# A quarter of the column terms by products over runs instead of gathers, and one comparison for a group's one-hot

## What is computed

```python
for l in range(3):
    f1 = relu(x[row] @ nb_W[l] + nb_b[l])
    f2 = relu(x[col] @ self_W[l] + self_b[l])
    h = relu(concatenate([f1, f2], axis=1) @ att1_W[l] + att1_b[l])
    log_alpha = (h @ att2_W[l] + att2_b[l])[:, 0]
    mask = clip(sigmoid(log_alpha) * (ZETA - GAMMA) + GAMMA, 0.0, 1.0)
    rowsum = segment_sum(mask, row) + 1e-06
    d_inv_sqrt = clip(rowsum ** (-0.5), 0.0, 10.0)
    vals = mask * d_inv_sqrt[row] * d_inv_sqrt[col]
    x = segment_sum(vals[:, None] * x[col], row)
    out = out + x
x = layernorm(x_in + out)
```

## Time and profile before

| | |
|---|---|
| median of 3 runs | 12707.59 us (12700.92 to 12740.07) |
| span of the profiled execution | 9111.0 us; no other time of that execution is given |
| median less span | 3596.6 us |
| PE, PEld busy | 5650.8 us, 5151.5 us |
| DVE, ACT, POOL busy | 6736.5 us, 3666.1 us, 5960.7 us |
| three layers' phase A | 6274.8 us of the span |
| three layers' phase B | 1907.1 us of the span |
| granted clock, mean | 0.623 |

### The profile page before, as it was taken

The page is one execution under the profiler, slowest core; times in us unless marked ns, Lnnn a source line. Parts: engine busy times, 40 slices in busy tenths (PEclk is TensorE's granted clock), DMA queues, the critical chain, the costliest instruction groups (busy, mean ns, idle before and its releaser), DMA issues.

```text
span 9111.0 us, 203370 instructions
## 1 busy us (share of the span) xinstructions
PE 5650.8 (62%) x43467; PEld 5151.5 (57%) x43630; DVE 6736.5 (74%) x29039; ACT 3666.1 (40%) x8663; POOL 5960.7 (65%) x6294
## 2 busy tenths in 40 slices
PE   3135555555558996555555557998555555555996
PEld 1135555545548885555555556887555555555886
DVE  8877777777777877777777777877777777776788
ACT  0013322322227883322322325885322322323886
POOL 0017777777775656777777776665777777776664
PEclk7565555555558996555555557998555555555998
DMA  1014444444456664444444446665444444445665
GB/s 24 0 48 135 132 130 131 132 130 130 133 128 206 213 206 130 132 131 130 132 130 131 132 130 176 210 212 156 132 130 130 133 130 131 132 130 146 213 211 161
DMA packets 1122388, 1272.27 MB, mean 140 GB/s; under 512 B 648596, under 2 KB 652724, under 8 KB 1122356
## 3 DMA queue, kind: packets, MB, share of 16 engines
q1 hardware_dynamic: 922676, 903.51, 32.1%
q0 software_dynamic: 199680, 368.45, 16.7%
HBM read 868.11 MB, written 403.23 MB: 140 GB/s over the span
## 4 chain that ended last, share of the span: by engine, by line
POOL 44%; issue 23%; PE 22%; DVE 8%; DMA 1%; ACT 1%; POOLq 0%; DVEq 0%; ACTq 0%; SPq 0%
POOL got L526 22%; PE bank L552 12%; POOL k_hot L526 11%; POOL g_hot L526 10%; PE bank L685 6%; DVE acc L946 2%; DVE acc L947 2%; PE bank L653 1%; PE bank L690 1%; PE bank L610 1%; PE bank L601 1%; PE bank L576 1%; DMA k_x<-kept_x 1%; DMA k_hot<-qx_table,index 0%; DVE acc L909 0%
## 5 line engine op out<-in xcount | busy, mean ns | idle before, releaser
L653 PE MATMUL bank<-p_all,onehot_t 128*128 x10032 | 2301.5, 424 | 1752.4 <-issue 1731.8
L653 PEld LDWEIGHTS bank<-p_all,onehot_t 128*128 128x128 f32 x10032 | 2186.8, 330 | 1803.4 <-issue 1803.4
L526 POOL DMA_INDIRECT got<-qx_table,index x2496 | 2376.4, 952 | 784.9 <-issue 780.3
L539 POOL DMA_INDIRECT got<-y_table,index x1248 | 1187.3, 951 | 798.8 <-issue 431.5
L798 ACT ACTIVATE small<-small 128x8 f32<-128x8 f32 x624 | 130.2, 209 | 3813.9 <-DVE small L1080 3813.9
L526 POOL DMA_INDIRECT k_hot<-qx_table,index x1248 | 1181.3, 947 | 393.7 <-issue 377.5
L526 POOL DMA_INDIRECT g_hot<-qx_table,index x1248 | 1185.6, 950 | 380.6 <-issue 380.6
L552 PE MATMUL bank<-mask,onehots 128*128 128x3 bf16 x4992 | 669.8, 184 | 986.1 <-DVE mask L1091 986.1
L552 PEld LDWEIGHTS bank<-mask,onehots 128*128 128x128 bf16 x4992 | 516.0, 104 | 1250.7 <-issue 1145.5
L1118 DVE SCALAR_TENSOR_TENSOR p_all<-iota_b,col_hi,bank 128x104 f32<-128x104 bf16 x3768 | 953.9, 317 | 341.5 <-PE bank L685 335.4
L1056 DVE TENSOR_SCALAR onehots<-iota_b,rows_b 128x128 bf16<-128x128 bf16 x5016 | 888.7, 280 | 48.0
(11 more groups left out here) (167 smaller groups left out, 8859.7 us busy)
## 6 DMA issues: line engine op xcount, KB each, us to landing
onehot_t<-look_hot SPq DMA_DIRECT2D x474, 256.0 KB
row_hot<-onehots SPq DMA_DIRECT2D x468, 256.0 KB, 3.6
k_x<-col_rows SPq DMA_DIRECT2D x318, 256.0 KB, 3.6
kept_x<-got SPq DMA_DIRECT2D x312, 256.0 KB
look_hot<-k_x SPq DMA_DIRECT2D x312, 256.0 KB, 2.1
hot_in<-row_hot SPq DMA_DIRECT2D x312, 256.0 KB
k_x<-kept_x SPq DMA_DIRECT2D x312, 256.0 KB
look_new<-row_hot SPq DMA_DIRECT2D x159, 256.0 KB
```

The costliest lines, as they stand in the source:

```text
L526: pool.indirect_dma_start(got[j][:, k, :], None, qx_table, bass.IndirectOffsetOnAxis(ap=index[j][:, k:k + 1], axis=0)).then_inc(a_got[j], 16)
L539: pool.indirect_dma_start(got[j][:, k, 0:HID], None, y_table, bass.IndirectOffsetOnAxis(ap=index[j][:, k:k + 1], axis=0)).then_inc(g_got[j ...
L653: last = mm(bank_p[h][:, k, :], onehot_t[h][:, k, :], p_all[:, ds(ids[k], 1), :].rearrange("p o d -> p (o d)"), start=True, stop=True)
```

## The change

**Fewer gathers.** The fourth group of each quad (j = 3) no longer gathers its Q. Its 1024 edges are cut into runs, stretches of one tile whose columns lie in one block of nodes. After the sort by row and column, the groups are ranked by their number of runs, and the 52 with the fewest are moved to the fourth place of the quads; at most 72 runs, here slots, stand for each. A slot's product multiplies a one-hot of the lanes of its edges (`slot_hot`, zero for edges of other runs) by the block of Q that the slot names, kept in SBUF as `q_res`, and adds to `bank[7]` at its tile. Block and tile of three slots are packed in one int32 word, which PE reads into a register and takes apart (`column_terms`). SP broadcasts the slots' lanes to all partitions (`load_slots`), DVE compares them with the partition number (`build_slots`). Nine rounds of eight slots make a quad's 72: rounds 0 to 2 in the group j = 0, 3 to 5 in j = 1, 6 to 8 in j = 2.

**One comparison.** A group has one one-hot, `hot[j]`, from `build_onehot`, for both of its uses.

**Besides.** The sort key also holds the column's block; finding the runs (nine times MAX and MATCH_REPLACE), ranking, and 36 gathers of column rows run once ahead of the layers. `block_of` and `spot_of` become rows of one int32 tile, `tile_at`. acc holds `q_res` in phase A, and POOL clears it by one memset ahead of phase B, in place of ACT step by step.

```diff
+    ROUNDS = 9
+    SLOTS = ROUNDS * U
+    SLOT_BITS, PER_WORD = 10, 3
+    WORDS = SLOTS // PER_WORD
+    RUNS = TILES + BLOCKS * (BLOCKS - 1)
+    ALL_GROUPS = 2 * PARTS
+    GROUP_EDGES = U * PARTS
+    PICKS = SLOTS // 2
+    CHUNK = PICKS // 3
...
-        block_of = sb("block_of", [1, TILES + AHEAD], mybir.dt.int16)
-        spot_of = sb("spot_of", [1, TILES + U], I32)
+        tile_at = sb("tile_at", [64, TILES + AHEAD], I32)
+        block_of, spot_of = tile_at[0:1, :], tile_at[32:33, :]
...
-        hot_a, hot_b = ([onehots[:, h * U:(h + 1) * U, :] for h in (first, first + 1)] for first in (0, 2))
+        hot = [onehots[:, j * U:(j + 1) * U, :] for j in range(4)]
...
+                def load_slots(b, r, made):
+                    if made is not None:
+                        sp.wait_ge(x_made, l * (ROUNDS * QUADS) + (b * ROUNDS + made))
+                        sp.sem_inc(sp_go, 1)
+                    sp.dma_start(slot_in[r % 3], slot_lanes[ds(b * SLOTS + r * U, U), :].rearrange("k e -> (k e)")
+                                 .partition_broadcast(PARTS)).then_inc(x_in[r % 3], 16)
...
+                        if j == 0:
+                            sp.wait_ge(x_used[0], l * (slots_used(0) * QUADS) + b * slots_used(0))
+                            sp.sem_inc(sp_go, 1)
+                            sp.dma_start(slot_word[0:1, :], slot_words[ds(b, 1), 1, :]).then_inc(w_in, 16)
+                            for r in range(3):
+                                load_slots(b, r, 0 if r == 0 else None)
                         load_columns(b, j + 2)
-                        sp.wait_ge(a_hotb, l * (GROUPS + 1) + (b * 4 + (j + 1)))
+                        sp.wait_ge(a_hot, l * (GROUPS + 2) + (b * 4 + (j + 1)))
                         sp.sem_inc(sp_go, 1)
                         sp.dma_start(row_hot[ds((b * 3 + j) * PARTS, PARTS), :],
-                                     hot_b[j % 2].rearrange("p k m -> p (k m)")).then_inc(a_hotst[j % 2], 16)
+                                     hot[j].rearrange("p k m -> p (k m)")).then_inc(a_hotst[j], 16)
+                        if j < 2:
+                            for r in (3 * j + 3, 3 * j + 4):
+                                load_slots(b, r, r - 2)
                         sp.wait_ge(a_got[j], (l * QUADS + b + 1) * GOT)
                         sp.sem_inc(sp_go, 1)
                         sp.dma_start(kept_x[ds((b * 3 + j) * PARTS, PARTS), :].rearrange("p (k d) -> p k d", k=U),
...
+            pool.wait_ge(s_place, 1)
+            for h in range(2):
+                pool.indirect_dma_start(
+                    sorted_keys, bass.IndirectOffsetOnAxis(ap=ranks_i[:, 2, h:h + 1], axis=0),
+                    sorted_of[:, h * GROUP_EDGES:(h + 1) * GROUP_EDGES], None
+                ).then_inc(s_scat, 16)
+            pool.wait_ge(s_nodest, 16)
+            pool.wait_ge(s_unpacked, 1)
+            for i in range(PICKS):
+                pool.indirect_dma_start(
+                    picked_rows[i // CHUNK][:, i % CHUNK * PARTS:(i % CHUNK + 1) * PARTS], None, node_rows,
+                    bass.IndirectOffsetOnAxis(ap=pick_row[:, i:i + 1], axis=0)
+                ).then_inc(s_picked[i // CHUNK], 16)
             pool.wait_ge(s_edges, 1)
...
-                    for j in range(4):
-                        pool.wait_ge(a_idx[j], l * (QUADS + (j < 3)) + (b + 1))
+                    for j in range(3):
...
+                pool.wait_ge(m_rows, l + 1)
+                pool.sem_inc(pool_go, 1)
+                pool.memset(acc[:, :, :], 0.0).then_inc(k_zero, 1)
...
+                        p_block = p_all[:, ds(ids[k], 1), :].rearrange("p o d -> p (o d)")
+                        if read:
+                            last = mm(bank_p[h][:, k, :], onehot_t[h][:, k, :], p_block, start=True, stop=True)
+                        else:
+                            last = plus(bank[7][:, k * HID:(k + 1) * HID], onehot_t[h][:, k, :], p_block)
...
+                def column_terms(b, j):
+                    n = l * QUADS + b
+                    if j == 0:
+                        pe.wait_ge(n_q, node_done(l, 0, NODE_STEPS - 1))
+                        pe.wait_ge(w_in, (n + 1) * 16)
+                        pe.sem_inc(pe_go, 1)
+                    pe.load(word, slot_word[0:1, j * U:(j + 1) * U])
+                    for r in range(3 * j, 3 * j + 3):
+                        pe.wait_ge(x_made, n * ROUNDS + (r + 1))
+                        for i in range(U):
+                            at, part = divmod((r - 3 * j) * U + i, PER_WORD)
+                            bits = pe.snap(word[at], min_val=0, max_val=BASE - 1) >> SLOT_BITS * part
+                            k = bits & U - 1
+                            s = nc.s_assert_within((bits >> 3) & PARTS - 1, 0, NB - 1,
+                                                   skip_runtime_bounds_check_because="a column's block is below BLOCKS")
+                            last = plus(bank[7][:, ds(k * HID, HID)], slot_hot[r % 2][:, i, :],
+                                        q_res[:, ds(s, 1), :].rearrange("p o d -> p (o d)"))
+                        last.then_inc(x_used[r % 2], 1)
...
-                with pe.Fori(0, GROUPS // 2) as b:
-                    for j in range(2):
-                        g = b * 2 + j
-                        row_terms(1 - j, g + 1, a_sum, l * GROUPS + g)
-                        turn_hot(j, g + 2)
-                        at = [pe.snap(r, min_val=0, max_val=BLOCKS - 1) for r in blk[j]]
-                        pe.wait_ge(a_hotb, l * (GROUPS + 1) + (g + 1))
+                with pe.Fori(0, QUADS) as b:
+                    for j in range(4):
+                        g = b * 4 + j
+                        if j == 2:
+                            column_terms(b, j)
+                            row_terms(1, g + 1)
+                        else:
+                            row_terms(1 - j % 2, g + 1, a_sum, l * GROUPS + g)
+                        turn_hot((j + 2) % 4, g + 2)
+                        if j == 0:
+                            pe.wait_ge(a_sum, l * GROUPS + g)
+                            clear(bank[7])
+                        if j < 2:
+                            column_terms(b, j)
+                        at = [pe.snap(r, min_val=0, max_val=BLOCKS - 1) for r in blk[j % 2]]
                         pe.wait_ge(a_m3, l * GROUPS + (g + 1))
                         for k in range(U):
-                            last = plus(bank_r[:, ds(at[k] * 4, 3)], hot_b[j][:, k, :], mask3[j][:, k, :])
...
-                        to = (j + 3) % 4
-                        act.wait_ge(a_add[to], l * QUADS + (b + (j > 0)))
-                        if to < 3:
-                            act.wait_ge(a_kept[to], (l * QUADS + (b + (j > 0))) * 16)
-                        a.copy(index[to][:, :], col_id[:, ds((g + 3) * U, U)]).then_inc(a_idx[to], 1)
+                        if j > 0:
+                            to = j - 1
+                            act.wait_ge(a_add[to], l * QUADS + (b + 1))
+                            act.wait_ge(a_kept[to], (l * QUADS + (b + 1)) * 16)
...
+            for r in range(ROUNDS):
+                eight = picks[:, 0, r * U:(r + 1) * U]
+                link(v.max(eight, pair[r % 2]))
+                link(v.match_replace(pair[(r + 1) % 2], eight, pair[r % 2], 0.0))
...
+                    v.tensor_copy(q_res[:, of_step(s), :], bank[4 + j % 2][:, :].rearrange("p (b d) -> p b d", d=HID))
...
-                def build_hot(to, rows, g, n, free, signal, stored=None):
-                    v.tensor_copy(rows[:, :], row_lo[:, ds(g * U, U)]).then_inc(a_rows, 1)
-                    dve.wait_ge(*free)
-                    if stored is not None:
-                        dve.wait_ge(stored[0], stored[1] * 16)
-                    dve.wait_ge(a_rows, l * (2 * GROUPS + 3) + (n + 1))
-                    for k in range(U):
-                        last = v.tensor_scalar(to[:, k, :], iota_b[:, :], rows[:, k:k + 1], None, ALU.is_equal)
-                    last.then_inc(signal, 1)
+                def build_hot(j, g, summed_up, stored):
+                    dve.wait_ge(a_row, l * (GROUPS + 1) + summed_up)
+                    if j < 3:
+                        dve.wait_ge(a_hotst[j], (l * QUADS + stored) * 16)
+                    build_onehot(hot[j], row_lo[:, ds(g * U, U)]).then_inc(a_hot, 1)
+                def build_slots(b, r):
+                    h = r % 2
+                    dve.wait_ge(x_in[r % 3], (l * (3 * QUADS) + (b * 3 + (r // 3 + 1))) * 16)
+                    dve.wait_ge(x_used[h], l * (slots_used(h) * QUADS) + (b * slots_used(h) + r // 2))
+                    v.tensor_scalar(slot_hot[h].rearrange("p k m -> p (k m)") if h == 0 else
+                                    slot_hot[h][:, :, :].rearrange("p k m -> p (k m)"),
+                                    slot_in[r % 3], part_f[:, :], None, ALU.is_equal).then_inc(x_made, 1)
+                dve.wait_ge(s_lanest, 96)
```

(24 more changed lines are left out.)

253 lines of the change are left out of this document (199 added, 54 removed).

## The result

The changed kernel takes 16,987.65 us (median of 4 runs, 16,966.37 to 17,021.72), the kernel before, beside it, 12,709.72 us (4 runs, 12,700.92 to 12,740.07): a ratio of 1.3366, 95% interval 1.3344 to 1.3388. I had forecast slower, 15,990 us, in a range that ended at 16,900. The side was right, the size 998 us short, and the time lies 88 us outside the range.

What follows compares the result with a forecast made beforehand. Phase A was taken as bound by POOL's gathers before and PE's sequencer after: (60.5 - 40.2) us x 156 quads + 115 = +3280 us on the 12,707.6 us median, 15,990 us; range 12,700 to 16,900.

Steps and rivals of the forecast that it cites:

- What bounds now: Phase A of the kernel before: bound by POOL's 32 gathers a quad, 40.2 us a quad.
- Register instructions, 94 to 106 ns each: PE's sequencer: five ahead of each slot product make a slot 0.525 us, 72 slots 37.8 us a quad.
- The array is not the limit: PE's array in the slots: 0.46 us a product at the lower clock, 0.24 at the upper, below 0.525 a slot.
- POOL and DMA are hidden: Phase A after: POOL's 24 gathers take 30.2 us a quad, DMA gains about 1.8 MB in 60 us; neither bounds.
- The int32 load: PE's load of eight block numbers: 591 ns instead of 2222 ns as int16, a gain of 1.6 us a group.
- The quad of 60.5 us: Phase A after: sequencer 57.9 us plus 2.6 of array time a quad, range 59.4 to 62.6, against 40.2 before.
- the array's own time: Last two groups of a quad, where no slots follow: adds 1.5 us at the upper clock, 4.7 at the lower; 2.6 taken.
- The single comparison is worth nothing: DVE in phase A: one comparison saves 8 us a quad, but PE's sequencer hides it, so no gain in time.
- The prologue, +105: Work ahead of the layers, with 36 gathers on POOL: 70 to 140 us more, 105 taken.
- The 3597 us: Timed median minus profiled span of the kernel before: assumed around the span or in unchanged parts, so the change adds 3280 us.
- Rival 1: The missing 3597 us are POOL's gathers, each slower in timed runs: centre 12,750 us, chance 0.22.
- Rival 3: The missing time is spread evenly, all engines slower by 1.395 in timed runs: 17,280 us, chance 0.1.

Runs made afterwards that it cites:

- e4: Changed kernel with one slot product a round (nine a quad) in place of eight, everything else kept: 12,771.17 us, ratio 1.003.
- e18: Changed kernel with 36 semaphore increments more a quad on TensorE's own queue: 17,525.36 us, ratio 1.3776.
- e3: Changed kernel with the 72 slot products at fixed addresses, without word loads or register instructions ahead of them: 14,128.37 us, ratio 1.1092.
- e2: Kernel before with only the single comparison in place of eight for each group's one-hots: 12,237.36 us, ratio 0.9611.
- e14: Changed kernel with the single comparison undone (a cast and eight comparisons a group again): 17,364.96 us, ratio 1.3644.
- e11: Changed kernel with 128 semaphore increments a queue ahead of the layers, moving all later code: 17,270.1 us, ratio 1.3506.
- the second profile: Kernel before, unchanged, timed and profiled again: 12,739.34 us, ratio 1.0006, span 12,718.5 us.
- e5: Kernel before with TensorE's phase A loop written over a quad (four groups) instead of two groups: 12,700.15 us, ratio 0.9992.
- e15: Kernel before with VectorE's phase A loop written over two quads: 12,719.94 us, ratio 0.9995.
- e9: Kernel before with 64 semaphore increments ahead of the layers on each of five queues, moving later code: 12,793.07 us, ratio 1.0003.
- e10: Kernel before with 128 semaphore increments ahead of the layers on each of five queues, moving later code: 12,810.31 us, ratio 1.0018.
- e12: Changed kernel with TensorE's phase A loop written over two quads: 17,025.14 us, ratio 1.3388.
- e6: Kernel before with 32 semaphore increments more a quad on ScalarE: 12,707.92 us, ratio 0.9995.
- e7: Kernel before with 24 semaphore increments more a quad on SyncE: 12,717.9 us, ratio 1.0.
- e16: Changed kernel with 36 semaphore increments more a quad on ScalarE: 17,050.13 us, ratio 1.341.
- e17: Changed kernel with 36 semaphore increments more a quad on VectorE: 17,062.28 us, ratio 1.3411.

## Why the prediction was right in direction and short in size

*What bounds now* failed for the timed runs. "Phase A is bound by POOL's 32 gathers" holds in the execution of the earlier trace rows, and there alone. In an execution like the timed ones a quad takes 54.3 us, not 40.2, POOL waits, VectorE is first in the chain, and in e4 a quarter fewer gathers won nothing.

*Register instructions, 94 to 106 ns each.* About right: 93 ns net in e18, and in the undisturbed slots of the packed trace (from 2063.4 us) the plain and fused ones of L676 mostly start 92 to 104 ns before the next instruction. A slot came to 0.576 us against 0.525, mostly since the first fused operation of each (L811) takes 84 ns, not 46. Eight rounds at 4.61 us and one at 3.50 are 40.4 us, where I had 37.8: 2.6 us a quad short.

*The array is not the limit, and POOL and DMA are hidden.* Right: e3's 0.43 us a slot is the array's; from e3 to the changed kernel, register work, loads and more steps add 18.7 us a quad. One round of the nine did go at the array's pace (3.50 us). The int32 load was 594 ns, as taken.

*The quad of 60.5 us.* It is 80.9. Of the 20.4 us, 13.5 are steps in the slots, 2.6 the slots themselves, and 4.3 the rest of the groups. About 2.1 of those 4.3 are the clock: I took 2.6 us for the array's own time, nearer the upper level, and 4.7 was my figure for the lower; the granted clock was 0.50 in phase A of all three layers, though PE was busy 3240 of 4214 us. I took the profiled execution, which had hardly any steps, as a model of the timed ones. This term was missing, and the top of my range had no room for it.

*The single comparison is worth nothing.* Wrong in the kernel before (3.9%, e2), where VectorE leads the chain and loses its steps with the comparisons. In the changed kernel e14 says 2.1%, of which a move of code may do half (e11); I leave the cause open.

*The prologue, +105.* Right: +100.9 us.

*The 3597 us.* **This is the step that failed**: "if they lie around the span, or in parts that the change leaves alone, the change adds 3280". Between the first profile and the second, the span grows by 3607.5 us. Some 1335 of them lie in the three phases B (1082.0 against 636.9 us), which the change does leave alone. But phase A of the second profile has 14.1 us a quad more than the 40.2 of the earlier trace rows, 2200 us, and these the change does not keep: the 20.4 of its own quad stand in their place. The difference of the two errors, 6.4 us x 156, is some 1000 us, what the median was beyond the forecast (998). That the forecast came this near is luck: two omissions, one on each side, nearly cancel. Against the true quad of 54.3 my quad of 60.5 would have meant +6.2 x 156 + 115, an estimate of 13,790 us. Rival 1 is refuted by the gathers' 952 ns. Rival 3, an even spread, gave 17,280 and came nearer in number, not in cause: phase A of before was slower by 1.35, phase B by 1.7, the sort and POOL's gathers not at all. I gave it 0.1, which was too little, and the range should have held it.

*What stays open:* what a step is, and which queue's steps set the quad of the kernel before. In the changed kernel it is TensorE's: it holds 72% of the chain and hardly waits, and its two stretches and the quad get longer together in e11 and e14. In the kernel before, TensorE's steps fell by half (e5), VectorE's fell (e15) or grew (e9, e10), and the time stayed; without VectorE's (e2) some 11 of 14 us remain. SyncE has the most steps there, and no run took them away.

The steps don't follow the number of passes throughout: once a pass on TensorE in e5, not so on VectorE in e15 and in the slots of e12. More instructions without work on waiting queues hardly change them (e6, e7, e16, e17). The Trainium skill (Runtime: NRT & Kernel Launch, Instruction fetch mechanics) has it that a taken branch to code outside the loaded window stalls the queue until it is fetched. The trace of e12 agrees: with transfers on the instruction queue its branch takes 5.4 us, against 0.21 in the changed kernel. The steps are something else, or not that alone: in the phases A of all runs but e12 and e15 hardly an instruction transfer runs (one, in e11, past the first 100 us of each), and the steps go on.

One thing the packed traces do show: the queues step on one beat. In the first layer's phase A of before's second profile, take the long register, semaphore and DMA-issuing instructions (0.67 to 0.72 us) of TensorE and SyncE. Of 365 pairs, one from each queue, that start within 1.8 us of each other, all lie 0.0, 0.7 or 1.4 us apart (to 0.05 us); in the changed kernel it is 367 of 391. That a common supply serves them by turns fits this and is not shown; what it supplies is open.

## What to carry to other kernels

Compare the profile's span with the timed median before anything else. If they differ by a quarter, the profiled execution is not like the timed ones, and its bound may not be theirs: profile again first. A product whose address a queue works out from packed bits costs the queue's instructions, here five at about 0.1 us, 0.58 us a product against 0.43 of array; 72 of these (40 us) don't pay for eight gathers of 1.25 us (10 us). Split a change into its parts: here the cheap part won 4% alone, and the whole lost 34%. And look at the trace of an experiment whose time did not move: in e12 two changes of some 2.5 us a quad hid each other.
